# Removing the memset behind every gather, and the waits for it, in a three-layer graph kernel

## The reference

```python
def _rgcn_layer(x, W, SW, b, src, dst, rel):          # layers 1 and 2
    xt = jnp.einsum('nd,rde->rne', x, W)
    agg = jax.ops.segment_sum(xt[rel, src], dst, num_segments=x.shape[0])
    return jax.nn.relu(agg + x @ SW + b)
...
x = _layernorm(x + two_rgcn_layers(x))
...
feat = jax.nn.relu(x @ W1 + b1)                        # layer 3
h = feat * d_invsqrt
agg = jax.ops.segment_sum(h[src], dst, num_segments=N)
x = _layernorm(x + (feat - agg * d_invsqrt) @ W2 + b2)
```

## Time and profile before

| | |
|---|---|
| median of 3 runs | 7126.02 us (7123.88 to 7126.11) |
| the profiled execution's own time | 7141.85 us |
| its span (first to last instruction) | 7140.1 us |
| POOL busy | 5849.0 us, 82% of the span |
| PE (TensorE matmul) busy | 3398.9 us, 48% |
| DVE (VectorE) busy | 1707.3 us, 24% |
| ACT busy | 692.0 us, 10% |
| DMA, mean busy share of the 16 engines | 0.19 to 0.20 through most of the span |
| mean granted TensorE clock | 0.643 of full speed |

### The profile page before, as it was taken

One profiled execution on the slowest core, in us unless ns is written; L12 is line 12 of the kernel. 1 busy time (PEld: TensorE's weight loads), 2 busy tenths in 40 slices (PEclk: granted clock), 3 DMA queues, 4 the chain that ended last, 5 costly groups with the idle time before them and its releaser, 6 DMA issues.

```text
span 7140.1 us, 55913 instructions
## 1 busy us (share of the span) xinstructions
PE 3398.9 (48%) x12908; PEld 2515.0 (35%) x12909; DVE 1707.3 (24%) x2844; ACT 692.0 (10%) x1395; POOL 5849.0 (82%) x9940
## 2 busy tenths in 40 slices
PE   4455445554445655555554555554333333333333
PEld 3333333333333433333333333344333333333333
DVE  5333333333333312222222222221111111111111
ACT  2111111111111211111111111110000000000000
POOL 8888888888888788888888888878888888888887
PEclk7667666776667767777777777775555555555555
DMA  2111111111111212212222122221111111111111
GB/s 67 52 51 51 50 51 52 50 50 51 51 52 52 53 51 57 57 55 56 58 56 56 55 57 57 56 59 51 53 53 52 52 54 52 52 53 54 52 52 53
DMA packets 197671, 382.92 MB, mean 54 GB/s; under 512 B 84402, under 2 KB 93406, under 8 KB 197622
## 3 DMA queue, kind: packets, MB, share of 16 engines
q0 software_dynamic: 159456, 326.88, 17.5%
q1 hardware_dynamic: 36496, 54.67, 2.2%
q10 hardware_dynamic: 1670, 0.85, 0.0%
HBM read 356.43 MB, written 25.65 MB: 54 GB/s over the span
## 4 chain that ended last, share of the span: by engine, by line
POOL 78%; issue 20%; PE 1%; POOLq 1%; DMA 0%; DVE 0%; ACT 0%; DVEq 0%; SPq 0%; ACTq 0%
POOL rows L802 63%; POOL pause L806 15%; PE bank L965 0%; PE bank L990 0%; POOLq L112 0%; POOL rows L772 0%; PE bank L299 0%; DMA rows<-x_d,idx 0%; POOLq L788 0%; PE bank L1214 0%; PE bank L286 0%; POOLq L796 0%; DMA rows<-in_x_dram,idx 0%; POOLq L812 0%; DMA rows<-h_d,idx 0%
## 5 line engine op out<-in xcount | busy, mean ns | idle before, releaser
L990 PE MATMUL bank<-r_S,rows 128*128 128x128 f32 x6644 | 1361.7, 388 | 2125.9 <-DMA rows<-in_x_dram,idx 1065.1
L990 PEld LDWEIGHTS bank<-r_S,rows 128*128 128x128 f32 x6644 | 1259.3, 292 | 2271.9 <-issue 2271.6
L802 POOL DMA_INDIRECT rows<-in_x_dram,idx x1661 | 1587.6, 956 | 449.9 <-issue 258.2
L802 POOL DMA_INDIRECT rows<-x_d,idx x1647 | 1573.4, 955 | 444.0 <-issue 253.9
L802 POOL DMA_INDIRECT rows<-h_d,idx x1640 | 1565.0, 954 | 366.9 <-issue 272.0
L1214 PE MATMUL bank<-r_S,rows 128*128 128x64 f32 x3322 | 767.8, 424 | 1468.3 <-DMA rows<-h_d,idx 1462.0
L1214 PEld LDWEIGHTS bank<-r_S,rows 128*128 128x128 f32 x3322 | 726.2, 330 | 1513.7 <-DMA rows<-h_d,idx 925.2
L806 POOL MEMSET pause<- 128x128 f32 x4948 | 1097.1, 222 | 4.0
L1051 DVE TENSOR_TENSOR r_S<-bank,key 128x1792 f32<-128x1792 f32 x238 | 480.4, 2019 | 1219.8 <-PE bank L990 1219.2
L917 ACT COPY r_agg<-bank 128x512 f32<-128x512 f32 x476 | 278.2, 584 | 3961.9 <-PE bank L965 2066.5
L1271 DVE TENSOR_TENSOR acc<-acc,bank 128x64 f32 x238 | 52.9, 222 | 1920.2 <-PE bank L1214 1904.4
(11 more groups left out here) (151 smaller groups left out, 1384.4 us busy)
## 6 DMA issues: line engine op xcount, KB each, us to landing
rows<-in_x_dram,idx POOLq DMA_INDIRECT x1661, 2.6
rows<-x_d,idx POOLq DMA_INDIRECT x1647, 3.5
rows<-h_d,idx POOLq DMA_INDIRECT x1640, 2.5
d_xr<-in_x_dram SPq DMA_DIRECT2D x54, 218.0 KB
x_d<-d_yr SPq DMA_DIRECT2D x27, 218.0 KB
d_x1r<-x_d SPq DMA_DIRECT2D x27, 218.0 KB
h_d<-d_hr SPq DMA_DIRECT2D x27, 218.0 KB
part_d<-d_pr SPq DMA_DIRECT2D x27, 218.0 KB
```

What stands on the lines that cost most here:

```text
L802: pool.indirect_dma_start(out=self.c.rows[:, self.place(s), :], out_offset=None, in_=self.table[:, :], in_offset=bass.IndirectOffsetOnAxis ...
L990: mm = pe.matmul(agg_ps[j][:, bass.ds(offs[j * KG + k], TK)], c.rows[:, g.place(h * KG + k), :], S[:, pb, j * KG + k, :], start=False, sto ...
```

## The change

The memset behind each gather is gone, and with it the buffer `pause`, the semaphore `paused`, all waits for it, the `gate` behind each of these waits, and the increments that stood in for skipped groups. The gathers, their order, `lead` with its three values, the waits at the head of a pair and `early` are as before.

```diff
@@ build
-        c.pause = sb("pause", [P, PT, P])
@@ Gathers.__init__
-        self.rest = PAIR if then is None else 1
-        self.paused = sem("paused")
@@ Gathers.run
-        rest = self.rest
-
         def iteration(q, i, part, set_of, skip=0, lead=PR):
             at = set_of * UN
             for p in part.pairs:
                 if (p + 1) * PT <= skip:
-                    pool.sem_inc(self.paused, PAIR // rest)
                     continue
                 pool.wait_ge(self.idx_ready, (q * (IT + 1) + i) * PR + p + 1)
                 pool.wait_ge(self.summed, self.pairs_summed(q, i, p + PR - lead))
                 gate(pool, self.c.passed)
                 for h in range(p * PAIR, (p + 1) * PAIR):
-                    if (h + 1) * KG <= skip:
-                        if h % rest == rest - 1:
-                            pool.sem_inc(self.paused, 1)
-                        continue
-                    if h % rest == 0:
-                        pool.wait_ge(self.paused, q * (NG // rest) + i * (RING // rest) + h // rest + 1)
-                        gate(pool, self.c.passed)
                     for k in range(part.of(h)):
                         s, slot = h * KG + k, h if k < halves(part, h) else RING + h % PAIR
                         if s < skip:
                             continue
...
                         ).then_inc(self.landed[slot], 16)
-                        ins = pool.memset(self.c.pause[:, s % PT, :], 0.0)
-                    if h % rest == rest - 1:
-                        ins.then_inc(self.paused, 1)
...
         pool.sem_inc(self.cleared, 1)
-        pool.sem_inc(self.paused, 1)
         one_round(0, EARLY[self.turns])
...
-        pool.wait_ge(self.paused, rounds * (NG // rest) + 1)
-        gate(pool, self.c.passed)
         if self.then is not None:
             self.early(pool, rounds, stored)
```

## The result

The changed kernel takes **6254.42 us** (median of 4 runs, 6254.1 to 6255.27), the kernel before 7125.6 us in the runs beside it (4 runs, 7123.88 to 7126.11). The ratio is 0.8778, with an interval of 0.8763 to 0.8793. The forecast was 6305 us, in a range of 6235 to 6430: the main mechanism was right, the size 51 us too high.

A forecast was written before the change was run, and what follows sets the result against it. The bound is POOL's own stream of gather, memset and gap, 4948 times. Span 7140.1 - 822 (stream 7088 to 6266) - 1.3 + 1 = 6318; + 1.75 - 15.8 = 6304, stated as 6305 us, range 6235 to 6430.

The forecast's parts named there:

- The write: Behind each of 4948 gathers on POOL: removing the memset gives back 0.09 us, not 0.39, a gain of 448 us.
- The wait: At 589 group or pair starts, POOL's wait for its own memset adds 0.64 us; removing it gains 377 us.
- rival 1: Pair heads on POOL stay expensive, each of 353 keeping its 0.64 us: +226 us, 6531 us; chance 0.07.
- The long gaps: On POOL, 69 gaps of 1.07 us, at each sum's 114th gather and every 70 after, stay: 62 us.
- The long gathers: In POOL's stream, gathers longer than 0.953 us stay as today and add 10 us.
- POOL's way into the early gathers: At the ends of sums, POOL's way into `early` loses a memset wait of 0.64 us twice: -1.3 us.
- wait for the store of h: At a sum's end POOL may arrive before the wide chunk's store has ended: 0 to 4 us, taken as 1.
- The subtraction of 15.8 us: From span to time: the profiled execution of before was 15.8 us above its runs' median, so 15.8 is taken off.
- rival 2: POOL's step of 1.251 us does not hold, falling back to 1.342; only the waits' 377 are won: 6749 us; chance 0.05.
- rival 3: TensorE becomes the bound, its lag passing the lead by 5 us in each of 87 iterations: 6740 us; chance 0.03.
- rival 4: VectorE's two-input SBUF instructions hold gathers up, 58 in the tails: at most 22 us more, 6327 us; chance 0.06.
- rival 5: Slower: a bare gather stream fills the queue and each gather waits for a landing, up to 12,900 us; chance 0.03.

The follow-up runs named there:

- the run with the writes alone: Kernel before with every memset kept, but each group waits for the write of the group before last, which is always met: 6682.53 us, ratio 0.938.

## Why the prediction was right, and where it was off

*What bounds the kernel.* Right. The kernel was bound by POOL's own stream and still is. The parts add up to the kernel before: 6254 + 428 (writes, by the run with the writes alone) + 377 (589 waits of 0.64 behind a write) + 62 (69 long gaps of 0.90, both by the rows of before) = 7121 us, against 7125.

*The write, 448 us.* Right: 428 measured. The early gathers, two short stretches without a write, had shown the step of the whole new stream within 0.003: 1.251 against 1.248.

*The wait, 377 us.* Right. But for the one at the start of sum 3, no head of a pair costs more than the gap of 0.30, so rival 1 has fallen. The same wait without a write before it costs 0.505, since the gap that it replaces is longer.

*The long gaps, +62 us.* **This is the step that failed**: "They are tied to a count of gathers, so I keep them". They are tied to one, but they were bare only in the second gather behind a wait, and 62 us of the forecast were for gaps that did not come. With the waits gone, the trace has none of them. The bound of -62 was in the range. The earlier trace rows gives only the gaps; that each stands just behind a group's start could have been read from the same timeline, and so could that no long gap stands anywhere else.

*The other terms.* The long gathers were kept at 10 us; 27 of them pass 1.02 us, against 26 before, and what they take beyond 0.953 adds up to 11.7 us. POOL's way into the early gathers was to lose 0.64 at each sum and lost more: the gap fell from 2.43 to 0.30 at sum 2. So at sum 3 POOL came earlier than forecast, and its 2.08 there are a wait for the store of h of about 1.8, forecast at 1 us. The gap of 2.05 behind it, the wait for the end of sum 2, was not in the forecast. The gathers' median times to landing, 2.6, 3.5 and 2.5 us in the three sums, are those of before, although one is now issued every 1.25 us. TensorE at 62% was as forecast. One reading of the prediction was wrong without effect on the sum: `mix` took its 14.94 us not at the low clock but at a granted clock of 1.00, the 2.4 GHz level:

```profile
2357.00:2373.00 16.00, 15.66 (x20) 3.84 (x20) 6.38 (x7) 0.28 (x1) 12.89 (x23) 1.00 0.17 45
```

*The sum.* The span was forecast at 6318 and is 6252.4, 66 us less. The long gaps account for 62 and the step for 15 (4948 times 1.2514 - 1.2484). Against them stand 11 us more than forecast: 5 in the stream beside the steady step, of which 1.8 are the wait for the end of sum 2, and 6 or 7 outside of the rows of L789 (58.5 us, where 7140.1 - 7088 had left 52).

*From span to time.* The subtraction of 15.8 us took off what the profiled run of before was longer than its median. The changed kernel's profiled run took 6254.18 us, within 0.3 of its median, so the whole 51 us are in the sum. The excess of the profiled run of before lay in its steps: inside the groups it went 1.3391 us from gather to gather, where the run with the writes alone, with the same instructions there and within 0.2 us of its own median, went 1.3354. Over 4948 gathers that is 18 us. The 1.2514 was read in the same long run, so the subtraction and the step that is 15 us too long cancel. What is left is 62 us of long gaps, less the 11. Why that run was longer is not known.

*The rivals.* The step held over 4948 gathers (rival 2); TensorE's sums held POOL up nowhere in the changed kernel, whose only waits are the two at the start of sum 3 (rival 3). The long gathers cost hardly more than before (rival 4): the contention that the Trainium skill describes in "SBUF — State Buffer", section "Who interferes with whom", is seen in single gathers, as in the earlier trace rows, but is not worth a term here, since all long gathers together cost 11.7 us. In the tails of the changed kernel 8 gathers take 1.33 to 1.47 us, and each starts within the first 0.2 us of an instruction of VectorE with two SBUF inputs; most of the 58 such instructions meet no gather in that way. No gap but the three single ones passes 0.6 us, so nothing is seen of a full queue (rival 5).

## What to carry to other kernels

An engine that only issues transfers should not be made to wait for its own last instruction: here it cost 0.5 to 0.64 us each time, and it also laid bare an extra step that otherwise does not show. A small instruction between two others may cost far less than its busy time, since it fills a gap that is there anyway, so read the gap without it before its busy time is counted as a gain. And where rare long gaps come at a fixed count, look at what stands just before each of them; a count alone does not say that they stay.

## What the runs showed of the hardware that was not expected

- An indirect gather costs POOL nearly the same for 128 rows and for 64: 0.946 + 0.305 us and 0.909 + 0.305. By this a faster kernel would need fewer gathers; none was tried.
- At every 70th gather of 128 rows (84th of 64 rows) the gap on POOL is 0.9 to 0.99 us longer if POOL has just stood waiting, for itself or for another engine, and the usual one if it has not. That POOL's issuing side has extra work there, which it otherwise does ahead, fits these runs; the profile does not show that work.
- A memset of 0.12 us between two gathers costs 0.006, one of 0.22 costs 0.09.
- The same kernel took 7125, 7277 and 7297 us on different chips. On the two slower ones, two variants that were expected to be faster were 1.7 to 2.6% slower than it, with TensorE going in single steps. The cause stays open.
